# The router of the last chunk in the first expert steps, and the large blocks fixed one chunk earlier

## What is computed

```python
for i in range(2):                      # attention part
    n = layer_norm(out) * ln_w[i] + ln_b[i]
    k, v, r = n @ Wk[i].T, n @ Wv[i].T, sigmoid(n @ Wr[i].T)
    state[t] = 0.95 * state[t-1] + 0.05 * (k * v)[t]
    out = out + (r * state) @ Wo[i].T
x = layernorm(h + out)
top_v, top_i = top_k(x @ Wg.T, 2); probs = softmax(top_v)     # router
for e in range(8):                      # experts
    g = silu(x @ W1[e].T) * (x @ W2[e].T)
    y += (g @ W3[e].T) * sum(probs * (top_i == e))
x = layernorm(x + y)
```

## Time and profile before

| | us |
|---|---|
| timed runs: median (lowest to highest of 3) | 1214.69 (1208.7 to 1215.05) |
| the profiled execution's own time | 1203.26 |
| its span, first to last instruction | 1201.4 |
| TensorE busy | 1087.7 (91%) |
| VectorE busy | 912.7 (76%) |
| ScalarE busy | 617.2 (51%) |
| GpSimd busy | 666.7 (55%) |
| mean granted TensorE clock | 0.958 of 2.4 GHz |

### The profile page before, as it was taken

One profiled execution on the slowest core, in us unless ns is written; L12 is line 12 of the kernel. 1 busy time (PEld: TensorE's weight loads), 2 busy tenths in 40 slices (PEclk: granted clock), 3 DMA queues, 4 the chain that ended last, 5 costly groups with the idle time before them and its releaser, 6 DMA issues. The chain is left out here.

```text
span 1201.4 us, 22049 instructions
## 1 busy us (share of the span) xinstructions
PE 1087.7 (91%) x6624; PEld 956.4 (80%) x6624; DVE 912.7 (76%) x2050; ACT 617.2 (51%) x1019; POOL 666.7 (55%) x560
## 2 busy tenths in 40 slices
PE   6999999999999998849999999999999999999900
PEld 5778887777777787638888888888888999999900
DVE  5688888888888888736876666777776778888736
ACT  3444444444444443335454555565565666666528
POOL 1111544545454544667666666676684777776434
PEclk9899999999999999859999999999999999999955
DMA  4011222111121121156766656777785889989569
GB/s 158 18 53 53 54 54 54 54 53 53 53 53 53 53 53 36 36 151 169 175 164 153 162 139 154 204 219 183 195 225 150 215 230 258 233 240 238 100 199 379
DMA packets 80243, 164.34 MB, mean 137 GB/s; under 512 B 27568, under 2 KB 44976, under 8 KB 79920
## 3 DMA queue, kind: packets, MB, share of 16 engines
q1 hardware_dynamic: 49968, 127.72, 34.0%
q0 software_dynamic: 30208, 35.81, 16.5%
HBM read 118.78 MB, written 44.70 MB: 136 GB/s over the span
## 5 line engine op out<-in xcount | busy, mean ns | idle before, releaser
L1177 POOL DMA_INDIRECT x_acc<-fy_sb,pair_out x136 | 259.6, 1909 | 116.8 <-issue 51.0
L1367 PE MATMUL fring<-fxh,fw_hi 128*128 128x256 f32 (+1 forms) x704 | 234.5, 333 | 5.0 <-DVE fxl L1281 1.9
L1369 PE MATMUL fring<-fxh,fw_lo 128*128 128x256 f32 (+1 forms) x704 | 233.8, 332 | 0.0
L1368 PE MATMUL fring<-fxl,fw_hi 128*128 128x256 f32 (+1 forms) x704 | 233.1, 331 | 0.0
L1197 ACT ACTIVATE fw_hi<-w_raw 128x1024 fp32r<-128x1024 f32 x156 | 163.6, 1054 | 97.3 <-PE fy L1412 88.6
L1259 DVE TENSOR_TENSOR fw_lo<-w_raw,fw_hi 128x1024 fp32r<-128x1024 f32 x156 | 189.4, 1218 | 14.7 <-ACT fw_hi L1197 14.2
L545 POOL TENSOR_TENSOR rs<-ve,neg_half 128x4 f32<-128x4 f32 x48 | 55.6, 1159 | 256.4 <-DVE nm L632 256.4
L98 POOL DMA_INDIRECT xg<-x_src,pair_in x136 | 155.4, 1143 | 75.0 <-issue 42.2
L88 POOL DMA_INDIRECT slot_list<-pairs,slot_u x128 | 145.9, 1140 | 50.5 <-issue 34.8
L869 PE MATMUL ring<-xh,w_hi 128*128 128x512 f32 x384 | 160.8, 419 | 2.2 <-issue 2.0
L1410 PE MATMUL fy<-fw_hi,gh 128*128 128x256 f32 x544 | 155.7, 286 | 0.0
(11 more groups left out here) (149 smaller groups left out, 2012.1 us busy)
## 6 DMA issues: line engine op xcount, KB each, us to landing
w_raw<-w_ffn SPq DMA_DIRECT2D x156, 512.0 KB, 4.8
x_in<-h SPq DMA_DIRECT2D x16, 512.0 KB, 3.3
x_src<-x SPq DMA_DIRECT2D x16, 512.0 KB, 4.6
x_acc<-x SPq DMA_DIRECT2D x16, 512.0 KB, 5.8
acc<-x_acc SPq DMA_DIRECT2D x16, 512.0 KB, 7.1
out<-o SPq DMA_DIRECT2D x16, 512.0 KB, 6.0
xg<-x_src,pair_in POOLq DMA_INDIRECT x136
x_acc<-fy_sb,pair_out POOLq DMA_INDIRECT x136, 4.7
```

The costliest lines, as they stand in the source:

```text
L1177: nc.gpsimd.indirect_dma_start(x_acc, bass.IndirectOffsetOnAxis(pair_out[j][:, q, 0:1].bitcast(U32), 0), y[j][:, q, :], None, compute_op=A ...
L1367: nc.tensor.matmul(out, hi, rows_hi, start=dc == 0, stop=False)
L1368: nc.tensor.matmul(out, hi, rows_lo, start=False, stop=False)
L1369: last = nc.tensor.matmul(out, lo, rows_hi, start=False, stop=dc == DC - 1)
```

## The change

- The large blocks are counted from 13 chunks in place of 14 (`EARLY`), so 18 of them instead of 20; the table is made in step 15. Two more large blocks (`MORE`, a fourth kind with a table of its own) are taken from the counts of all chunks and stand behind the mixed stretch, where the last two large blocks stood. The number, sizes and order of the 52 blocks stay.
- The attention phase ends after step 17. The last chunk's router moves into the expert phase: its transposes behind those of block 0 (step -1), its gates between units 1 and 2 of step 0, `choose_last` at the end of VectorE's step 0, its ranks between units 1 and 2 of step 1, `place_last` in VectorE's step 1 ahead of `x_lo`, its two sigmoids at the end of ScalarE's step 1. TensorE waits for `place_last` before the output product of step 1.
- Of chunk 13's scatters three stay in step 17, ahead of the gathers of block 0, which now stand ahead of the `rstd` of the last chunk. The other five are issued in step -1, chunk 14's eight in steps 0 and 1, chunk 15's eight in steps 2 and 3.
- SP loads the pairs of blocks 0 and 1 in step 17, after the scatters and stores of 13 chunks. The waits for the stores of all chunks move from the end of the attention phase to SP's step 8.
- In step -1 ScalarE's `x_hi` stands ahead of the second weight cast. Two more stores of zeros clear the rows of the last two chunks in `x_src`. Two more steps of the expert phase (22 and 23) are written out. The router's tiles move to buffers that outlive the attention phase.

The diff, cut:

```diff
-EARLY = CHUNKS - 2
+EARLY = CHUNKS - 3
...
-SIZES = [Q] * 10 + [Q, 1] * SINGLES + [Q] * (BIG - SINGLES - 10) + [2] * PAIRS
-KIND_BLOCKS = (BIG, SINGLES, PAIRS)
+MORE = 2
+KIND_OF = [0] * 10 + [0, 1] * SINGLES + [0] * (BIG - SINGLES - 10) + [3] * MORE + [2] * PAIRS
+KIND_BLOCKS = (BIG, SINGLES, PAIRS, MORE)
...
@@ rest_counts
+    shifted(nc, dve, k, k.full[:, :], k.used[:, :], 0, CH.bit_length() - 1)
+    table_link(dve, k, nc.vector.tensor_tensor(k.full[:, :], k.full[:, :], k.taken[:, 0, 0:E], ALU.subtract))
+    take(nc, dve, k, 3, MORE)
+    table_link(dve, k, nc.vector.scalar_tensor_tensor(k.tiles[:, :], k.taken[:, 3, 0:E], -float(Q), k.tiles[:, :],
+                                                      ALU.mult, ALU.add))
@@ rest_starts
-    skips(nc, dve, k, 1)
-    skips(nc, dve, k, 2)
+    for kind in (1, 2, 3):
+        skips(nc, dve, k, kind)
@@ attention_phase
-        LAST = CHUNKS + 4
+        LAST = CHUNKS + 2
...
-            for dst in (x_src, x_acc):
-                sp.dma_start(dst[TOKENS:TOKENS + CH, :] ... z[:, :, :]).then_inc(s_padst, 16)
+            for dst, row in ((x_src, TOKENS), (x_acc, TOKENS), (x_src, TOKENS - CH), (x_src, TOKENS - 2 * CH)):
+                sp.dma_start(dst[row:row + CH, :] ... z[:, :, :]).then_inc(s_padst, 16)
...
                 for par in range(2):
-                    sp.wait_ge(s_sc[par], SCAT * (EARLY // 2))
-                sp.dma_start(kept.pair_in[0][:, :, :], slot_list[bass.ds(slot_row, CH), :] ...
+                    sp.wait_ge(s_st[par], 32 * ((EARLY + 1 - par) // 2))
+                    sp.wait_ge(s_sc[par], SCAT * ((EARLY + 1 - par) // 2))
+                for b in range(2):
+                    sp.dma_start(kept.pair_in[b][:, :, :], slot_list[bass.ds(slot_rows[b], CH), :] ...
...
-            for par in range(2):
-                sp.wait_ge(s_st[par], 32 * (CHUNKS // 2))
...
                 if at(s, CHUNKS + 1):
                     open_scatter(s, half, j)
-                    scatter(s, j, 0, 6)
+                    scatter(s, j, 0, 3)
+                    gather_rows(nc, pool, kept, x_src, s_met, 0, 0, Q)
                     rstd(2, s - 2)
-                    scatter(s, j, 6, 2)
                     return
...
-                if at(s, CHUNKS + 2):
-
-                    scatter_pairs(nc, kept, slot_list, j, 0, Q)
-                    gather_rows(nc, pool, kept, x_src, s_met, 0, 0, Q)
@@ expert_phase, run
-            loop(mixed + 4, mixed_end - 2)
-            peeled(mixed_end - 2, pairs_from + 4)
+            loop(mixed + 4, mixed_end - 4)
+            peeled(mixed_end - 4, pairs_from + 4)
@@ sync
                 if at(s, 8):
-                    sp.wait_ge(kept.s_table, 6)
+                    sp.wait_ge(kept.s_table, 8)
                     for par in range(2):
+                        sp.wait_ge(kept.s_st[par], 32 * (CHUNKS // 2))
                         sp.wait_ge(kept.s_sc[par], SCAT * (CHUNKS // 2))
@@ gpsimd
-            scatter_pairs(nc, kept, slot_list, 0, Q, Q)
+            def late_scatters(j, first):
+                if first == 0:
+                    if j == 1:
+                        pool.wait_ge(kept.s_sc[1], SCAT * (CHUNKS // 2 - 1))
+                        pool.wait_ge(s_last_prob, 1)
+                        pool.wait_ge(s_last_slot, 1)
+                    pool.sem_inc(s_met, 1)
+                    ids = kept.pairs[j][:, :, :, 0].bitcast(I32)
+                    nc.gpsimd.tensor_scalar(ids, ids, 2 * CH, None, ALU.add).then_inc(s_late_ids, 1)
+                    pool.wait_ge(s_late_ids, j + 1)
+                scatter_pairs(nc, kept, slot_list, j, first, Q)
...
-                if isinstance(s, int) and 0 <= s <= 1:
-                    scatter_pairs(nc, kept, slot_list, 1, s * Q, Q)
+                if at(s, -1):
+                    scatter_pairs(nc, kept, slot_list, 1, 3, 2 * Q - 3)
+                if isinstance(s, int) and 0 <= s <= 3:
+                    late_scatters(s // 2, s % 2 * Q)
@@ scalar
+                if at(s, 0):
+                    for dc in range(DC):
+                        act.wait_ge(s_last_t, dc + 1)
+                        nc.scalar.activation(kept.x1T[:, dc, :], flat_bank(dc), ACT.Copy).then_inc(s_last_x1T, 1)
                 if nxt:
                     w_half(0, s + 1, half + j, 1 - j, spot, 1)
+                if at(s, -1):
+                    x_hi(spot, 1)
...
+                if at(s, 1):
+                    act.wait_ge(s_last_gap, 1)
+                    act.wait_ge(kept.s_sc[1], SCAT * (CHUNKS // 2 - 1))
+                    nc.scalar.activation(kept.pairs[1][:, :, 0, 1], kept.gap[:, :], ACT.Sigmoid)
+                    nc.scalar.activation(kept.pairs[1][:, :, 1, 1], kept.gap[:, :], ACT.Sigmoid, scale=-1.0).then_inc(s_last_prob, 1)
+                    nc.scalar.activation(warm[:, :], zero[:, :], ACT.Silu)
@@ vector
+            def place_last():
...
+                dve.wait_ge(s_last_rank, 1)
+                link(4, nc.vector.tensor_tensor(k.slot[:, :, :], ranks, ...))
+                nc.vector.tensor_tensor(k.base[:, :], total, k.base[:, :], ALU.add).then_inc(s_last_base, 1)
+                link(5, nc.vector.tensor_tensor(k.own[:, :, :, :], k.sel[:, :, :, :], ...))
+                link(6, nc.vector.reduce_sum(k.slot_f[:, :, :], k.own[:, :, :, :], AX_X))
+                dve.wait_ge(kept.s_sc[1], SCAT * (CHUNKS // 2 - 1))
+                nc.vector.tensor_copy(k.slot_u[1][:, :, :], ...).then_inc(s_last_slot, 1)
+                dve.wait_ge(s_last_base, 1)
...
+                if at(s, 1):
+                    place_last()
                 if nxt:
                     x_lo(spot, 1)
...
+                if at(s, 0):
+                    choose_last()
...
                 if at(s, 3):
-                    fill_table(nc, dve, kept, 2)
+                    for kind in (2, 3):
+                        fill_table(nc, dve, kept, kind)
@@ tensor
                     for u in range(UNITS[spot.size(0)]):
                         hidden(s, j, u, spot)
+                        if u == 1 and at(s, 0):
+                            gates_last()
+                        if u == 1 and at(s, 1):
+                            ranks_last()
...
+                if at(s, -1):
+                    for dc in range(DC):
+                        for q in range(Q):
+                            last = nc.tensor.transpose(flat_bank(dc)[:, q * P:(q + 1) * P], kept.x1[:, 1, q, dc * P:(dc + 1) * P], ident[:, :])
+                        last.then_inc(s_last_t, 1)
+                if at(s, 1):
+                    pe.wait_ge(s_last_slot, 1)
+                    pe.wait_ge(s_last_base, 1)
```

176 lines of the change are left out of this document (125 added, 51 removed).

## The result

| | before | after |
|---|---|---|
| timed, median (lowest to highest), us | 1216.08 (1208.7 to 1220.83) | 1226.14 (1220.44 to 1233.81) |
| ratio to before, 95% interval | | 1.0099 (1.0077 to 1.0121) |
| profiled execution (span), us | 1203.26 (1201.4) | 1225.95 (1224.1) |
| first expert matmul, H0, us | 536.51 | 535.30 |
| steps 0 and 1; 2; 3; 4, us | 33.46; 18.77; 17.68; 17.32 | 46.65; 18.68; 23.72; 19.18 |

The kernel became about 1% slower, where 1211.0 us was forecast. (The interval is made from all timed runs; the two medians alone give 1.0083.) The two profiled executions stand 22.7 us apart and the medians 10: before's profiled execution is shorter than any of its timed ones, after's is near its median. So an account made from the two traces explains 22.7 us, and what before loses elsewhere in its timed executions is not shown by a trace.

A forecast was written before the change was run, and what follows sets the result against it. TensorE bounds it; its hole before the first expert matmul reaches the end one for one. Gain 7.3 + 1.8 - 1.85 - 0.5 - 1.1 - 2.0 = 3.65 us, as ratio 0.30%: 1211.0 us, range 1204 to 1217.

The forecast's parts named there:

- Part 1: Large blocks' table made in attention step 15: all its 4.2 us land on TensorE's wait for the second `y`.
- Part 2: Chain from chunk 12's last scatter to the expert phase: first expert matmul at 529.2 instead of 536.51, 7.3 us earlier.
- with the meeting of 2.1 us the expert phase begins at 525.3: End of attention: all engines meet 2.1 us after SP's last store is issued, so experts begin at 525.3 instead of 532.6.
- Part 3: Moved router inside expert steps: gates 1.85, ranks 0.5, slot wait 1.1, tables 2.0 us lost; GpSimd's later scatters nothing.
- the wait for `place_last`: Expert step 1: TensorE waits 1.1 us before its output product, ends 0.5 and 1.5.
- The paragraph on GpSimd: Scatters of chunks 14 and 15 moved into expert steps 0 to 3, delaying a gather 2.5, then 5 us: no cost.
- The tables: 25 more VectorE instructions in expert steps 1 to 3, 5.0 us, partly covered: 2.0 us lost, between minus 1.2 and 5.0.
- Part 4: Clock at expert start: full level back about 1 us behind the first expert matmul instead of 5, gaining 1.8 us.
- the reading by which the term would be 0: Clock at expert start: if transposes did not count as activity at all, the 1.8 us gain would be 0.
- No gain: Rival, chance 0.20: clock returns late (0 instead of 1.8), tables cost their full 5.0 us; about 1215.5 us.
- Slower: Rival, chance 0.10: late chunk 12 scatter and pair load make the chain 7.7 us later; 4.1 us slower, 1218.8 us.
- All three signs of being wrong: First expert matmul after 533; GpSimd `pair_in` wait of several us; TensorE waits on VectorE 3 us or more, steps 2-4.

The follow-up runs named there:

- e10: Changed kernel with the rest's tables in six small pieces ahead of the weighing and the sixteen late scatters moved to steps 3 to 6; ratio 1.0035 to before.
- e14: Changed kernel with `rstd` and four chunk 13 scatters ahead of the gathers, small table pieces, late scatters in steps 3 to 6; ratio 1.0022 to before.
- e16: Changed kernel with eight scatters, gathers, then `rstd`; late last stores; small table pieces; two late scatters per step in steps 0 to 7; 1211.43 us, ratio 0.997.

## Why the prediction was wrong, point by point

**Part 1** (4.2 us on the `y` wait) was right: 4.09 became 8.20 us.

**Part 2** failed in one step: "with the meeting of 2.1 us the expert phase begins at 525.3". I took the time between GpSimd's last operation and the next phase from before and carried it over as a constant. In before the indirect transfers, from 513.86 us on, had been running long when they ended, and the drain was short; in after the series begins only with the first gather, and the drain ends some 14 us behind that start, plus `rstd`. The phase came 531.71 - 525.3 = 6.4 us late, of the 7.3 that I had counted as gain. From SP's last issue (525.3) to the phase it was 6.4 us and not 2.1, so 4.3 are this step's. The other 2.1 are mostly the pair load: issued at 511.15 for 510.8, it landed at 515.27, 4.1 us later, where I took 2.7 and the median of the earlier trace rows was 4.4. Had the load come on time, at 513.5, the series and with it the drain's end would have come 1.8 us earlier and the phase at about 529.9, an estimate: still 4.6 us behind the forecast. That the drain holds the phase is shown by the one-series kernels, with an idle of 3.42 us in place of 10.17 and a phase that begins right behind ScalarE. Where it ends is a rule found afterwards in these traces, and why it ends there is open.

**Part 3**, what stands in steps 0 and 1, was right where nothing disturbs them: 34.7 to 34.95 us in four kernels against 33.46, hence 1.2 to 1.5 us where 1.85 + 0.5 + 1.1 - 1.8 = 1.65 was forecast. Of it, the wait for `place_last` is 0.80 us and not 1.1; TensorE without the late scatters:

```profile
566.25 0.38 PE L1528 MATMUL fy<-fw_hi,gh 128*128 128x256 f32 x1 [0.80 <-DVE slot_u L1368]
```

The paragraph on GpSimd ("Nothing, on both") failed. I asked only whom GpSimd's own delay would hold and not what the transfers do to others; in after the late reports, with the clock that fell in them, cost 46.65 - 34.80 = 11.9 us, by two single traces. It is the largest term of the loss, and no rival had it.

**The tables** were mis-sized: 2.0 us forecast, 5.0 as the upper end. Steps 2 to 4 lost 7.8 us in after, 6.7 in its repeat, and 5.1 without the late scatters, so about 5 us are the tables alone. "In the others about half of it is covered" is the failed sentence: the half had no row behind it but VectorE's idle time in a step, and the piece stands behind the last weighing, where VectorE has no slack before the next `gated`. In small pieces ahead of the weighing the cost is gone (steps 2 and 3 take 17.3 us in e10, e14 and e16), so cover was there, at another place.

**Part 4**, the clock, was right in size. TensorE alone, two-microsecond stretches of after (busy time, clock, DMA share, GB/s):

```profile
532.00:534.00 2.00, 2.00 (x11) 0.50 0.29 43
534.00:536.00 2.00, 1.94 (x10) 0.75 0.93 358
536.00:538.00 2.00, 2.00 (x11) 1.00 1.02 373
```

The 2.4 GHz level came back at about 535.0 us, 3.3 us after TensorE resumed and before H0. In the kernel without late scatters it came at 538.0, 4.6 us after resuming and 1.0 behind H0, as forecast. Over the seventeen traces of the changed kernel and its variants it came 3.2 to 5.6 us after TensorE resumed. The Trainium skill (TensorE: Matmul & The Clock Gate, Part 1) gives about 4 us into sustained matmul work, with half a microsecond either way. The traces here spread wider. In after TensorE had done nothing but the sixteen transposes when the level rose, so the reading by which the term would be 0 is out.

**The rivals.** "No gain" had the right engine for a part, with too small a price. (Its sum of -1.2 us makes about 1215.9, not 1215.5.) "Slower" had another cause in the main. All three signs of being wrong that I had named came: H0 behind 533, a `pair_in` wait of 6.30 us and a TensorE wait on VectorE of 3.42 us in step 3. With H0 1.2 us earlier and not 7.3, 11.9 us of late reports, 1.3 us that steps 0 and 1 take without them (34.80 against 33.46) and 7.8 in steps 2 to 4, the traces' 19.8 us come together. With the drain, tables and scatters arranged otherwise the kernel came to 0.997 and 0.9997; that the first is the ratio I had forecast is chance, since its steps still hold a late report and its end the longer drain.

**Open.** How the scatters delay reports, and why at varying places; what the drain waits for, at the end of both phases; why the pair load was issued anywhere from 507.4 to 517.4 us in the traces of the changed kernel and its variants; and where before loses what its timed executions take more than its two profiled ones (1203.26 and 1209.1 us against medians of 1210.43 to 1216.08).

## What to carry to other kernels

The gap between the last work and the next phase is not a constant: ask which engine's end closes the phase and what that engine had in flight, since here a shorter chain uncovered a drain that a longer one had hidden. Work hidden by an average idle share must be placed against the next instruction that somebody waits for; the same VectorE work cost 5 us behind the weighing and nothing ahead of it in small pieces. When transfers are moved beside others, price what they do to everyone's reports and not only the issuing engine's time.

## What the runs showed of the hardware

GpSimd's drain at the end of the attention phase lasted 9.1 to 12.8 us in thirteen traces in which a short series of indirect transfers (three or four) stood behind a pause, and was over 14 to 15.3 us behind that series' start: to GpSimd's next instruction it was 14.97 to 15.05 us with nothing behind the series, 15.47 with the id update and 16.29 to 16.32 with an `rstd`, whether the series was three scatters or four gathers. Where twelve transfers or more were issued in the last step or two it lasted 1.3 to 6.8 us and ended 0.4 to 1.0 us behind the last landing. The long series also have more transfers, and no run separates their number from their length; nor is it a rule for every phase, since at the end of the expert phase the drain was over 6.65 to 10.93 us behind the start of the last two adds.

A finished matmul's report can reach the other engines 4 to 11 us late, several steps of the counter at once, in steps with indirect scatters beside weight loads and gathers. Without the sixteen late scatters, in steps 0 to 2 of one execution, the hidden products' reports were at most 0.64 us late; those of the output products were 1.1 to 1.3 us late in the steps behind.
